# Reordering the second half's normalisation, output projection and expert work of a gated cross-attention kernel

## The reference

```python
delta = xattn(layernorm(x), ctx, mask)          # 16 heads of 16; masked softmax, clipped scores
delta = clip(residual_scale, 0, 0.3) * nan_clean(heads @ Wo.T + bo)
delta = (delta - mean) / sqrt(var + eps) * gamma + beta
x     = x + tanh(g_xattn) * delta
h     = layernorm(x)
p     = softmax(h @ router.T)                   # 8 experts; the best 2, made to sum to 1
y     = sum over the best 2 of p_e * ((up_e(h) * silu(gate_e(h))) @ down_e)
x     = x + tanh(g_ffn) * y
```

## Time and profile before

| | us |
|---|---|
| median of 3 runs | 257.62 (257.48 to 258.49) |
| the profiled execution's own time | 257.16 |
| its span in the trace | 255.3 |
| TensorE busy | 224.7 (88%) |
| VectorE busy | 180.1 (71%) |
| ScalarE busy | 146.1 (57%) |
| GpSimd busy | 55.4 (22%) |

### The profile page before, as it was taken

The page is one execution under the profiler, slowest core; times in us unless marked ns, Lnnn a source line. Parts: engine busy times, 40 slices in busy tenths (PEclk is TensorE's granted clock), DMA queues, the critical chain, the costliest instruction groups (busy, mean ns, idle before and its releaser), DMA issues.

```text
span 255.3 us, 7153 instructions
## 1 busy us (share of the span) xinstructions
PE 224.7 (88%) x2756; PEld 193.1 (76%) x2756; DVE 180.1 (71%) x456; ACT 146.1 (57%) x242; POOL 55.4 (22%) x90
## 2 busy tenths in 40 slices
PE   0889899469999999999999799958999399999994
PEld 0667688358888888988888688946799289899993
DVE  1788747663567897677778877893398877956754
ACT  2837667985446799699747872541643247316110
POOL 3381000011433342100002201371124534100000
PEclk9999999759999999999999999987899979999999
DMA  6999613096931799997993000300010000100101
GB/s 208 327 423 415 194 43 83 5 379 195 414 107 44 281 311 349 398 344 203 375 415 130 0 3 7 66 9 3 0 36 0 0 3 1 36 0 3 37 0 36
DMA packets 12867, 37.53 MB, mean 147 GB/s; under 512 B 2320, under 2 KB 10016, under 8 KB 10528
## 3 DMA queue, kind: packets, MB, share of 16 engines
q1 hardware_dynamic: 11728, 36.13, 39.6%
q10 hardware_dynamic: 1008, 0.92, 1.3%
q0 software_dynamic: 96, 0.00, 0.0%
HBM read 35.14 MB, written 0.92 MB: 141 GB/s over the span
## 4 chain that ended last, share of the span: by engine, by line
PE 58%; DVE 19%; issue 8%; ACT 6%; DMA 3%; POOL 3%; SPq 1%; DVEq 0%; ACTq 0%; POOLq 0%
PE bank L538 12%; PE bank L545 10%; PE bank L808 10%; PE bank L823 7%; PE bank L555 6%; PE bank L566 5%; DMA x_sb<-x_dram 3%; POOL guess L382 2%; PE bank L530 2%; ACT p L901 2%; PE bank L523 2%; DVE acc L1156 1%; DVE half_var L1084 1%; DVE stats L1092 1%; ACT L1021 1%
## 5 line engine op out<-in xcount | busy, mean ns | idle before, releaser
L808 PE MATMUL bank<-rowsT,gate_up 128*128 128x224 f32 x256 | 57.3, 370 | 0.0
L901 ACT ACTIVATE p<-bank,mask_bias,mask_scale 125x896 f32<-125x896 f32 x38 | 39.7, 1096 | 25.9 <-PE bank L555 25.9
L808 PEld LDWEIGHTS bank<-rowsT,gate_up 128*128 128x128 f32 x256 | 49.8, 198 | 2.2 <-issue 0.3
L538 PE MATMUL bank<-ctx_pair,wk 128*128 128x250 f32 x152 | 40.5, 411 | 10.0 <-DMA ctx_pair<-ctx_dram 7.5
L538 PEld LDWEIGHTS bank<-ctx_pair,wk 128*128 128x128 f32 x152 | 29.3, 203 | 15.4 <-issue 10.5
L545 PE MATMUL bank<-wv,ctx_pair 128*125 128x256 f32 x152 | 37.6, 391 | 0.0
L1021 ACT ACTIVATE silu<-bank 128x224 f32<-128x224 f32 x32 | 11.4, 357 | 44.5 <-PE bank L808 44.5
L1143 DVE TENSOR_SCALAR p<-p 125x912 f32<-125x912 f32 x38 | 27.4, 737 | 11.9 <-ACT p L901 11.9
L823 PE MATMUL bank<-down,act 128*112 128x256 f32 x128 | 34.5, 397 | 0.5 <-DVE act L1443 0.5
L545 PEld LDWEIGHTS bank<-wv,ctx_pair 128*125 128x125 f32 x152 | 29.7, 196 | 4.7
L913 ACT ACTIVATE ctx_all<-ctx_all 128x1500 f32<-128x1500 f32 x19 | 27.9, 1474 | 0.0
(11 more groups left out here) (158 smaller groups left out, 297.5 us busy)
## 6 DMA issues: line engine op xcount, KB each, us to landing
ctx_all<-ctx_dram SPq DMA_DIRECT2D x13, 1500.0 KB, 8.3
ctx_pair<-ctx_dram SPq DMA_DIRECT2D x38, 125.0 KB, 5.0
gate_up<-ctx_dram SPq DMA_DIRECT2D x3, 1500.0 KB, 10.4
gate_up<-gate_up_dram SPq DMA_DIRECT2D x1, 2048.0 KB, 12.4
down<-down_dram SPq DMA_DIRECT2D x1, 1024.0 KB, 14.4
num<-acc SPq DMA_DIRECT2D x16, 57.0 KB
x_sb<-x_dram SPq DMA_DIRECT2D x2, 448.0 KB, 6.6
out_dram<-x_sb SPq DMA_DIRECT2D x4, 224.0 KB, 2.3
```

The costliest lines, as they stand in the source:

```text
L538: mm = nc.tensor.matmul(bank[:, K_BANK, 2 * TT * m:2 * TT * (m + 1)], wk[:, k, P * m:P * (m + 1)], tile[:, :, k, :], start=(k == 0), stop= ...
L808: mm = nc.tensor.matmul(bank[:, GU_BANK[s], CHUNK * g:CHUNK * (g + 1)], gate_up[:, e, k, g, :], rowsT[:, k, CHUNK * c:CHUNK * (c + 1)], st ...
L901: nc.scalar.activation(p_tile[:, t].rearrange("t (j n) s -> t j n s", j=4)[:, :, :, 0:S], bank[0:TT, 0:4, DEN * t:DEN * (t + 1)].rearrange ...
```

## The change

Five things change, all in order and place; no product, no operation and no DMA is added or taken away.

- The transposes of quarter 0 go into bank 4 (keys) instead of bank 7, with semaphores of their own (`early_mm`, `early_out`); so they wait for the last copy of the keys and for the normalised rows, and no longer for the use of bank 7 ahead of them. In exchange the experts' first steps use banks 5 and 4 instead of 4 and 5.
- TensorE: the two spreads of half 1 stand behind `expert_out(4)` and `expert_out(5)`, ahead of the transposes of quarter 1, which stand behind `expert_out(6)`. The projection of quarter 2 stands behind `expert_out(7)`, with `expert_in(8)`, `route(1)` and `expert_in(9)` behind it; the projection of quarter 3 behind `expert_out(9)`. The transposes of quarter 2 stand behind `expert_out(13)`, and `expert_out(14)`, `expert_in(16)`, `route(2)`, `expert_out(15)`, `expert_in(17)` follow.
- VectorE: `inverses(1)` ahead of `gate(5)` and of `add_delta(0, 1)`; `totals(1)` and the first multiplication ahead of `h_offsets(0, 1)`; the rest as the diff shows.
- ScalarE: as TensorE; the exponentials of the router's quarters 1 and 2 stand behind `gate_silu(9)` and `gate_silu(17)`.
- GpSimd: `h_guess(1)` stands behind the addition of step 1.

```diff
-        GU_BANK = [4, 5] + [s % 4 for s in range(4 * NE - 2)]
-        D_BANK = [4, 5, 6]
+        GU_BANK = [V_BANK, K_BANK] + [s % 4 for s in range(4 * NE - 2)]
+        D_BANK = [V_BANK, K_BANK, PV_BANK]
...
-        USES = ["rank", "list", "masked0", "spread0", "out0_0", "out0_1", "hT0", "route0", "masked1", "hT1",
-                "spread1", "route1", "spread1b", "out1_0", "out1_1", "hT2", "route2", "hT3", "route3"]
+        USES = ["rank", "list", "masked0", "spread0", "out0_0", "out0_1", "route0", "masked1", "spread1",
+                "spread1b", "hT1", "out1_0", "route1", "out1_1", "hT2", "route2", "hT3", "route3"]
...
             for s in range(2 * NE):
-                if s == 1:
+                if s == 2:
                     h_guess(1)
...
+            def early_transposes():
+                pe.wait_ge(main.k_out, NTAIL)
+                pe.wait_ge(h_normal, 2)
+                transposes(bank[:, K_BANK], 0).then_inc(early_mm, 1)
...
                 if i == NOPT + 11:
-                    h_transposes(0)
+                    early_transposes()
...
             masked_sums(1)
-            for s in range(2, 4 * NE + 2):
+            for s in range(2, NE):
+                expert_in(s)
+                expert_out(s - 2)
+                if s == 6:
+                    use("spread1")
+                    spread_inverse(1, 0, misc(0, 2 * DEN)).then_inc(misc_mm, 1)
+                if s == 7:
+                    use("spread1b")
+                    spread_inverse(1, 1, misc(0, 2 * DEN)).then_inc(misc_mm, 1)
+            expert_out(6)
+            h_transposes(1)
+            expert_out(7)
+            project_out(1, 0)
+            expert_in(8)
+            route(1)
+            expert_in(9)
+            for s in range(10, 16):
+                expert_in(s)
+                expert_out(s - 2)
+                if s == 11:
+                    project_out(1, 1)
+            h_transposes(2)
+            expert_out(14)
+            expert_in(16)
+            route(2)
+            expert_out(15)
+            expert_in(17)
+            for s in range(18, 4 * NE + 2):
                 if s < 4 * NE:
                     expert_in(s)
                 expert_out(s - 2)
-                if s == 6:
-                    h_transposes(1)
-                if s == 7:
-                    use("spread1")
-                    spread_inverse(1, 0, misc(0, 2 * DEN)).then_inc(misc_mm, 1)
-                    route(1)
-                if s == 8:
-                    use("spread1b")
-                    spread_inverse(1, 1, misc(0, 2 * DEN)).then_inc(misc_mm, 1)
-                if s == 9:
-                    project_out(1, 0)
-                if s == 11:
-                    project_out(1, 1)
-                if s == 14:
-                    h_transposes(2)
-                if s == 15:
-                    route(2)
...
+            for s in range(2, NE):
                 gate_silu(s)
...
+                scale_expert(s - 2)
+            h_rows(1)
+            scale_expert(6)
+            misc_rows(1)
+            scale_expert(7)
+            gate_silu(8)
+            gate_silu(9)
+            exps_of_logits(1)
+            for s in range(10, 16):
+                gate_silu(s)
+                scale_expert(s - 2)
+                if s == 14:
                     h_rows(2)
...
```

More of the change, by code:

```diff
@@ L693, in h_transposes, with rows_ready @@
                 transposes(misc(0, 2 * CHUNK), c).then_inc(misc_mm, 1)
+            def rows_ready(c):
+                if c == 0:
+                    pe.wait_ge(early_out, 1)
+                else:
+                    pe.wait_ge(misc_out, USE[f"hT{c}"] + 1)
             def route(c):
                 use(f"route{c}")
+                rows_ready(c)
                 for t in range(2):
@@ L804, in expert_in @@
                 if e == 0:
-                    pe.wait_ge(misc_out, USE[f"hT{c}"] + 1)
+                    rows_ready(c)
                 for g in range(2):
@@ L942, in exps_of_logits, with early_rows @@
                 nc.scalar.activation(probs[:, 2 * c:2 * c + 2], logits[:, 2 * c:2 * c + 2], ACT.Exp).then_inc(e_out, 1)
+            def early_rows():
+                act_e.wait_ge(early_mm, 1)
+                nc.scalar.copy(rowsT[:, :, 0:CHUNK], bank[:, K_BANK, 0:2 * CHUNK].rearrange("p (k n) -> p k n", k=HALVES)
+                               ).then_inc(early_out, 1)
             def misc_rows(c):
@@ L1035, in _ @@
             gate_silu(1)
-            for s in range(2, 4 * NE):
+            for s in range(2, NE):
                 gate_silu(s)
-                if s == 6:
-                    h_rows(1)
-                if s - 2 < 2 * NE:
-                    scale_expert(s - 2)
-                if s == 6:
-                    misc_rows(1)
-                if s == 8:
-                    exps_of_logits(1)
-                if s == 13:
-                    h_rows(2)
-                if s == 14:
-                    misc_rows(2)
-                if s == 16:
-                    exps_of_logits(2)
-                if s == 20:
+                scale_expert(s - 2)
[10 more added lines that the diff above has]
+                if s == 14:
+                    h_rows(2)
+            misc_rows(2)
+            scale_expert(14)
+            gate_silu(16)
+            scale_expert(15)
+            gate_silu(17)
+            exps_of_logits(2)
+            for s in range(18, 4 * NE):
+                gate_silu(s)
+                if s == 18:
                     h_rows(3)
@@ L1468, in _ @@
             gate(4)
+            inverses(1)
+            gate(5)
             add_delta(0, 1)
-            gate(5)
-            h_offsets(0, 1)
-            inverses(1)
             gate(6)
             totals(1)
+            misc_mix(0, "spread1")
+            h_offsets(0, 1)
+            misc_mix(1, "spread1b")
             gate(7)
-            misc_mix(0, "spread1")
+            delta_parts(1, 0)
+            gate(8)
             shift_logits(1)
-            misc_mix(1, "spread1b")
-            gate(8)
+            delta_whole()
+            gate(9)
             expert_ranks(1)
+            gate(10)
             expert_weights(1)
-            gate(9)
-            delta_parts(1, 0)
-            gate(10)
-            delta_whole()
+            add_gains(1, 0)
             gate(11)
-            add_gains(1, 0)
-            gate(12)
             add_delta(1, 0)
             delta_parts(1, 1)
+            gate(12)
+            h_offsets(1, 0)
             gate(13)
-            h_offsets(1, 0)
+            delta_whole()
             gate(14)
-            delta_whole()
+            add_gains(1, 1)
             gate(15)
-            add_gains(1, 1)
+            add_delta(1, 1)
+            gate(16)
             shift_logits(2)
-            gate(16)
-            add_delta(1, 1)
+            h_offsets(1, 1)
             gate(17)
-            h_offsets(1, 1)
             expert_ranks(2)
```

6 lines of the change are left out of this document (2 added, 4 removed).

## The result

| | kernel before | changed kernel |
|---|---|---|
| first timing, median | 258.06 us (4 runs, 257.48 to 258.76) | 252.75 us (4 runs, 252.36 to 255.08) |
| ratio | | 0.9854 [0.9804, 0.9903] |
| second timing, median | 256.88 us (23 runs, 254.37 to 261.04) | 252.87 us (7 runs, 252.35 to 256.61) |
| ratio | | 0.9844 [0.9823, 0.9865] |
| profiled execution, its span | 257.16, 255.3 us | 252.65, 250.8 us |

The change makes the kernel 1.5% faster. The forecast was 251.4 us and a gain of 6.05 us on the profiled execution; measured are 252.75 us and 4.5 us on the profiled execution, 5.3 us between the medians of the first timing and 4.0 us between those of the second. In the ratios executions disturbed in the slow state are left out; the medians contain all.

A forecast was written before the change was run, and what follows sets the result against it. TensorE's queue bounds the kernel, held up by VectorE's list. New losses of 7.65 us plus 1.7 for the clock replace 15.1; with 0.3 at the start the gain is 6.05 us, forecast 251.4 us, range 247.2 to 255.8.

The forecast's parts named there:

- TensorE's standing in the second and third quarters is the loss: From expert_out(4) to expert_out(18), 55.86 us hold 40.7 us of work; 15.1 us lost standing, in smaller waits and low clock.
- The spots: New TensorE waits: second spread, transposes of quarter 1, then expert_out(12), (14), (15) and (18); 7.65 us in sum.
- The three last spots: TensorE waits ahead of expert_out(14), expert_out(15) and expert_out(18), for their gates: 0.45, 1.3 and 0.35 us.
- The clock: One low-clock stretch on TensorE, around the gaps at 169.5 to 174.3, charged at 1.7 us; bounds none and three.
- the other reading: TensorE's clock falls only after long pauses, so none of the new gaps lowers it; sum 1.7 us lower.
- First transposes: Quarter 0's transposes wait for normalised rows instead of VectorE's fix_raw; gain 0.3 us, between 0 and 0.4.
- The guess one addition later: GpSimd's h_guess(1) behind step 1 puts one more addition on add_gains(0, 1); cost 0.85 us on VectorE's list, bounds 0 and 1.1.
- DMAs of denominators and numerators: At VectorE's inverses(1) and totals(1), no wait for landing taken; other end a wait of 2 us in each.
- VectorE's list is the bound from the projection on: VectorE waits for quarter 2's projection at 177.4, then runs without pause, its list full from 177 to 213.
- 1: VectorE and clock kinder: additions miss delta_parts(1, 1) (2.0 us), no low stretch (1.7 us), or both; 247.0 to 249.3 us, 15%.
- 2: Low clock on TensorE after each larger gap, two stretches more than charged; 253.5 to 256 us, chance 18%.
- 3: Slower: TensorE's clock stays low from the spread to the third quarter, 172 to 196; 260 us, chance 9%.

The follow-up runs named there:

- e4: Changed kernel with GpSimd's additions of steps 8 to 15 taking in only the first channel of each row; median 250.44 us.
- e5: Changed kernel with spare TensorE products ahead of the second spread, the transposes of quarter 1 and expert_out(12); ratio 0.9734.
- e6: Changed kernel with h_guess(1) back behind the addition of step 0; ratio 0.9771.
- e1: Kernel before with only the first transposes moved into the bank of keys; ratio 0.9965.
- e3: Changed kernel with gate 12 put ahead of delta_parts(1, 1); ratio 0.9823.
- e2: Changed kernel with the third quarter's steps, from expert 10 on, in the old order on TensorE, ScalarE and VectorE; median 257.03 us, ratio 0.9997.
- a1_again: Changed kernel run once more, nothing altered; timed 4.0 us below the kernel before, profiled execution 256.19 us.
- f2: Changed kernel with guess back, projection of quarter 2 earlier, VectorE's gates and list reordered, two spare expert_out products; 247.75 us, ratio 0.9639.
- e9: Kernel before with spare TensorE products, three ahead of the transposes of quarter 1 and five ahead of those of quarter 2; ratio 0.9881.
- e7: Changed kernel with projection of quarter 2 ahead of expert_out(7) and quarter 1's transposes, VectorE reordered to match; median 253.04 us, ratio 0.9766.

## Why the prediction came out as it did

- *TensorE's standing in the second and third quarters is the loss.* Right. In the stretch 15.1 us of losses became 10.0; forecast were 9.35.
- *The spots.* Forecast 1.8, 1.2, 2.55, 0.45, 1.3 and 0.35 us; measured 1.71, 1.25, 2.48, 0, 0 and 0, with 0.19 at `expert_in(16)`, which the prediction had named as a sign of being wrong; it is small. The additions fell on `delta_parts(1, 1)` as charged (1.50 and 1.48 us), and e4 shows that they are the cause. In one place luck helped: `add_gains(1, 0)` was charged 1.1 us for an addition and met none, `add_delta(1, 0)` was charged 0.6 of one and lost 1.6 us (2.48 instead of 0.87), and the two errors nearly cancel.
- *The three last spots* were computed as if the low clock came only in the second quarter. There was a second low stretch at 199 to 203 us, and the slow TensorE came to those gates no earlier than the gates. e5, without low clock, has two of them: 0.15 and 1.14.
- *The clock.* One low stretch was charged at 1.7 us, and two came. The price is right all the same: without any low stretch (e5) the stretch is 1.65 us shorter. That is in part luck. The first low stretch held the projection up by 1.50 us, and the second, which was not charged, cost next to nothing, since TensorE was waiting for VectorE there anyway. What the prediction gave as the other reading, that only long pauses bring the clock down and that there would be no low stretch, did not come: both came after gaps of 2.48 us or less, shorter than the 2.97 and 4.57 us of before.
- *The miss of 0.6 us in the stretch* (10.0 lost, 9.35 forecast) is there at full clock too: 49.01 us in e5 against the 40.7 + 7.65 = 48.35 of the sum without its clock term. It arises ahead of the projection. The prediction let VectorE begin on it at 177.4, 12.1 us behind `expert_out(4)`; in e5 it began 12.66 us behind it, and from there the forecast had 36.45 us to `expert_out(18)` and e5 36.35. What the sum left out are TensorE's small stops, 1.7 us in the whole stretch of e6 and about 0.6 of it ahead of the projection.
- *The last step of the sum* has a slip: 251.1 plus the 0.46 of the median is 251.6, not 251.4.
- *First transposes* 0.3 us forecast, 0.4 measured, alone (e1) and in the changed kernel.
- *The guess one addition later* costs 0.85 us by the forecast; the standing at the second spread is 0.95 us shorter without it (e6).
- *DMAs of denominators and numerators*: no wait at `inverses(1)` or `totals(1)`, as assumed.
- *VectorE's list is the bound from the projection on*: e3 moved a wait and won nothing, e2 took the order away and lost it all, and the table above has the list at the same length in seven traces. Its two pauses, 0.58 and 0.51 us, are more than the none that was forecast.
- Of the rivals, 1 did not come; its condition that no low stretch comes was met in e5 and e6, where the profiled executions took 250.50 and 249.86 us, a little above its 247.0 to 249.3. Of 2, one low stretch more than charged came instead of two, and it cost almost nothing. 3 did not come: each low stretch ended within some 4 us in the profiled execution, though a1_again shows one of nearly 7 us, which made the stretch 1.65 us longer.
- The remaining miss of the profiled execution, 1.2 us, lies ahead of the first change. The prediction took that part as unchanged; its time scatters by more than that from trace to trace (the last section).

## What to carry to other kernels

When a gap in the bounding engine ends at another engine's instruction, add up that engine's whole list before moving the one instruction: moving a single gate turned a wait of 2.5 us into two of 1.0 and 1.5 (e3), while starting the list 4.4 us earlier, with the other edits of f2, made the stretch 4.6 us shorter. Price every instruction of the late engine with what a neighbour does to it at that moment; here eight additions on GpSimd made the stretch 4 us of 50 longer (e4). And look at the clock after each gap before trusting a moved product's length: the same projection took 1.98 us in one order and 3.67 in another.

## What the runs showed of the hardware that had not been expected

- The low clock does not follow from the length of one gap. After 2.48 us standing the clock fell in the changed kernel; after 2.50 us at the same place it did not fall in e6. After gaps of about 1.72 and 1.25 us around a spread and an `expert_out` it fell in five traces (changed kernel, a1_again, e2, e3, e4); after 0.76 and 1.25 it did not (e6). In e9 it fell with 0.79 us standing. What decides in the borderline cases stays open.
- In the changed kernel, in a1_again and in e7 TensorE stands 1.94 or 1.95 us ahead of the second spread of half 0, an instruction for which the profile names no releaser, and which the change does not touch. The other traces, the kernel before among them, have no such gap there. In the window of that gap (121 to 126 us) the DMA view of these three traces has one packet of the queue named `instruction`, while the data queue keeps the DMA engines full:

```profile
124.67 1.02 PE L677 MATMUL bank<-inv_den,spread 32*128 32x224 f32 x4 [1.94 <-issue]
```

```profile
q1 hardware_dynamic: 723, 1.99, 103.8%
q8 instruction: 1, 0.02, 1.2%
```

  The first row is from TensorE's timeline, the others are the queues (packets, MB, share of 16 engines) of the changed kernel in that window. None of the ten other traces has such a packet in this window, and none has the gap; e3 is among them, which differs from the changed kernel in one place of VectorE's list. That TensorE waited there for its instructions is likely, not shown; no experiment was made on it. Nor is it sure that this gap is the 1.2 us that the changed kernel lost ahead of all that was changed. The last product with `wk` starts at 140.48 us there and at 139.31 in the kernel before, but in the nine other traces without the gap it starts anywhere from 138.87 to 140.60.
